# Two block layers on one core: every fourth copy of turned exponentials moved from ScalarE to VectorE

## What is computed

```
q = w8a8(x, wq, bq)                       # 16 heads of 32, 100 rows
k, v = cond @ wk.T + bk, cond @ wv.T + bv # 361 rows
scores = einsum(q, k) / sqrt(32) + mask
attn = softmax(scores)
out = w8a8(attn @ v, wo, bo)
```

## Time and profile before

| | us |
|---|---|
| median of 3 runs | 718.23 |
| lowest and highest | 718.14, 722.27 |
| profiled execution | 719.32 |
| its span, first to last instruction | 717.4 |
| attention's masks and exponentials, first to last | about 338 to 485 |
| VectorE's masks (line 1184) | 128 x 531 ns |
| ScalarE's exponentials (line 605) | 128 x 607 ns |
| ScalarE's copies of turned heads (line 596) | 128 x 405 ns |

### The profile page before, as it was taken

The page is one execution under the profiler, slowest core; times in us unless marked ns, Lnnn a source line. Parts: engine busy times, 40 slices in busy tenths (PEclk is TensorE's granted clock), DMA queues, the critical chain, the costliest instruction groups (busy, mean ns, idle before and its releaser), DMA issues. The chain is left out here.

```text
span 717.4 us, 11182 instructions
## 1 busy us (share of the span) xinstructions
PE 527.6 (74%) x3590; PEld 373.8 (52%) x3590; DVE 367.5 (51%) x962; ACT 296.6 (41%) x631; POOL 180.0 (25%) x211
## 2 busy tenths in 40 slices
PE   0070569999999999548999999994172089999991
PEld 0040557677777777323776666672172055555540
DVE  5727747755865766263578878762521032222220
ACT  4056623444344343042798888891010022222220
POOL 1001013222322321104244444423104502222221
PEclk9995779999999999859899999997555589999996
DMA  8959600000000000310122222421402524455534
GB/s 334 423 177 348 206 0 12 11 0 11 11 0 11 11 0 1 125 21 23 29 80 87 81 89 91 131 84 42 173 0 67 153 50 88 88 90 89 90 44 121
DMA packets 23076, 62.60 MB, mean 87 GB/s; under 512 B 3938, under 2 KB 9858, under 8 KB 20986
## 3 DMA queue, kind: packets, MB, share of 16 engines
q1 hardware_dynamic: 18622, 53.47, 22.1%
q0 software_dynamic: 4416, 8.63, 7.5%
HBM read 46.40 MB, written 17.32 MB: 89 GB/s over the span
## 5 line engine op out<-in xcount | busy, mean ns | idle before, releaser
L605 ACT ACTIVATE pE<-sN,nmx 100x361 f32<-100x361 f32 x128 | 77.7, 607 | 6.0 <-DVE nmx L1184 5.6
L1184 DVE CUSTOM_DVE_ANT_0 sN<-ps,maskS 100x361 f32<-100x361 f32 x128 | 61.9, 531 | 14.6 <-PE ps L793 6.1
L932 PE MATMUL ps<-VS,hTe 118*128 x120 | 56.7, 609 | 5.5 <-ACT hTe L643 5.5
L801 PE MATMUL ps<-ident,pE 100*121 100x100 f32 x384 | 57.5, 282 | 1.8 <-ACT pT L596 1.3
L801 PEld LDWEIGHTS ps<-ident,pE 100*121 100x121 f32 x384 | 47.5, 188 | 21.5 <-issue 20.4
L506 POOL DMA_INDIRECT sums_out<-yb,backI x20 | 31.1, 1554 | 108.2 <-ACT yb L653 104.4
L596 ACT COPY pT<-ps 121x300 f32<-121x300 f32 x128 | 51.8, 405 | 13.2 <-PE ps L801 12.6
L1296 DVE TENSOR_TENSOR hb<-ps,b1B 128x352 f32<-128x352 f32 x20 | 10.5, 524 | 87.6 <-PE ps L918 87.6
L918 PE MATMUL ps<-CT,xT 128*128 x160 | 52.5, 472 | 2.0 <-DVE xT L1282 2.0
L918 PEld LDWEIGHTS ps<-CT,xT 128*128 128x128 f32 x160 | 31.1, 196 | 24.7 <-issue 12.5
L1065 DVE TENSOR_REDUCE tk<-h 100x1 f32<-100x512 f32 x32 | 20.0, 680 | 39.6 <-ACT h L556 39.5
(11 more groups left out here) (237 smaller groups left out, 1181.5 us busy)
## 6 DMA issues: line engine op xcount, KB each, us to landing
VS<-in_w SPq DMA_DIRECT2D x8, 1024.0 KB, 9.1
CT<-in_ctxT SPq DMA_DIRECT2D x8, 728.0 KB, 16.4
CT<-in_ew SPq DMA_DIRECT2D x8, 704.0 KB
VS<-in_ew SPq DMA_DIRECT2D x8, 672.0 KB
slots_in<-zeros SPq DMA_DIRECT2D x5, 1056.0 KB, 12.4
xin<-slots_in SPq DMA_DIRECT2D x20, 264.0 KB, 3.4
XR<-in_x SPq DMA_DIRECT2D x1, 1600.0 KB
summB<-summary_rows SPq DMA_DIRECT2D x8, 200.0 KB
```

What stands on the lines that cost most here:

```text
L605: act.activation(pE[0:S, q, 0:T], sN[0:S, q, 0:T], ACT.Exp, scale=-1.0, bias=nmx[0:S, h_:h_ + 1], accum_out=sums[0:S, j, h_:h_ + 1]).then_ ...
L801: mm = pe.transpose(ps[0:TC, 4 + r, c * S:(c + 1) * S], pE[0:S, h_ % HPC, c * TC:(c + 1) * TC], ident[0:S, 0:S])
L932: mm = pe.matmul(ps[:, 7 - j, :], hTe[0:EC, 1 - j, c, :], vs(e)[0:EC, c * D:(c + 1) * D], start=(c == 0), stop=(c == 2))
L1184: dve.tensor_tensor_reduce(out=sN[0:S, q, 0:T], in0=ps[0:S, q, 0:T], in1=maskS[0:S, j, 0:T], scale=-1.0, scalar=3.4e38, op0=ALU.add, op1=A ...
```

## The change

ScalarE no longer copies the turned exponentials of the last head of a group (heads 3, 7, 11 and 15 of a batch). VectorE does, by a new function `copy_last`, right behind its mask of the head five later: that of head 3 behind mask 8, of 7 behind mask 12, of 11 behind mask 0 of the next batch, of 15 behind its mask 4. The last two of all come after the loop. The semaphores and the places in pT are the same; only the engine and the place in its order differ.

```diff
@@ ScalarE, body @@
                     at_turn = behind(b, h_ - TURN, first)
-                    if at_turn:
+                    if at_turn and at_turn[1] % HPC < HPC - 1:
                         copy_turned(*at_turn)
@@ ScalarE, after the batches @@
-            for ht in range(HEADS - TURN, HEADS):
-                copy_turned(B - 1, ht)
+            copy_turned(B - 1, HEADS - TURN)
@@ VectorE @@
+            def copy_last(b, ht):
+
+                n = b * 8 + ht // 2
+                dve.wait_ge(sem("p_turned1"), after(n + 1))
+                dve.wait_ge(sem("mixed"), groups_mixed(b * KC + ht // HPC - 1))
+                dve.tensor_copy(pT[0:TC, ht % (2 * HPC)].rearrange("p c s -> p (c s)"), ps[0:TC, 5, 0:NT * S])\
+                   .then_inc(sem("p_copied1"), 1)
+
@@ VectorE, body, behind the mask of head h_ @@
+                    if h_ % HPC == 0 and b * HEADS + h_ > 4:
+                        copy_last(*divmod(b * HEADS + h_ - 5, HEADS))
                     if h_ in steps:
@@ VectorE, after the batches @@
+            copy_last(B - 1, HEADS - 5)
+            copy_last(B - 1, HEADS - 1)
             finish5(B - 2)
```

## The result

| | before | after |
|---|---|---|
| median, us | 718.35 (6 runs, 717.7 to 722.3) | 767.8 (6 runs, 758.3 to 777.3) |
| ratio to before | | 1.058, 95% interval 1.052 to 1.065 |
| span of the profiled execution | 717.4 | 773.1 |
| VectorE's copies into pT | 0 | 32 x 466 ns |
| ScalarE's copies into pT | 128 x 405 ns | 96 x 405 ns |

The change makes the kernel about 6% slower.

The account below looks back on a forecast made before the run. The prediction took the ring TensorE to VectorE to TensorE as the bound: 719.3 us profiled + 21.4 order + 1.8 clock = 742.5, less 1.1 for the median = 741.4, rounded to 742; range 731 to 762.

Parts of the forecast that it names:

- Direction and mechanism: Attention stage: slower, chance 0.93, since TensorE's second turn of a group waits for VectorE's copy behind a mask needing new scores.
- The chain: From a group's scores through mask, gap and VectorE's copy to the second turn: 1.03 + 0.46 + 0.47 + 0.14 = 2.10 us.
- the late mask: Group of head 9: mask 12 comes 2.18 us after the scores, so the turn starts at 3.25 us.
- The other estimate, 0.44: VectorE's copy out of PSUM by the Trainium skill's formula, 120 cycles plus columns at 0.96 GHz: 0.44 us.
- The sum of the order: Delays of TensorE's groups over all batches: 10.2 + 6.3 + 3.1 + 1.8 = 21.4 us; a steady batch 18.9 to 21.5.
- the first group loses nothing: Steady batch, scores at 418.40: the next pass already waited for VectorE until 2.53 us after them; after the change 2.50, loss 0.
- ScalarE's relief: ScalarE loses 32 copies, 13 us of busy time, but was already waiting for TensorE, so nothing is gained.
- VectorE's load: VectorE gains 32 copies, 15 us; later masks shift about 0.45 us, covered by TensorE being 0.9 us late.
- The clock, one fall at 1.8 us: TensorE's clock falls to half once more in the attention stage, costing 4.5 - 4.5/1.7 = 1.8 us.
- the thin one: Stretch from the scores at 424.13: TensorE's scores 0.87 and two turns about 0.9 us busy of 3.4, a further fall likely.
- The steady stretch with 2.37 us busy: Kernel before: a TensorE stretch with 2.37 us busy kept the full clock, taken as evidence against frequent falls.
- rival 2: TensorE's clock falls about once a batch or oftener, every group holding idle time; seven falls 13 us, 748 to 765, chance 0.30.

Follow-up runs that it names:

- experiment 4: Changed kernel with VectorE's four copies moved behind the mask of the group's last head, four heads later instead of five: 724.9 us, ratio 1.006.
- experiment 1: Changed kernel with clock-holding products added on TensorE ahead of each group's second turn, filling the new waits: 743.5 us, ratio 1.035.
- experiment 2: Changed kernel with only head 3 of each batch copied by VectorE, ScalarE copying the other 15: 740.4 us, ratio 1.030.
- experiment 5: Kernel before, with ScalarE's copy of heads 3, 7, 11 and 15 cut to 4 of 300 columns, nothing new on VectorE: 719.6 us, ratio 1.000.
- experiment 9: Kernel before, ScalarE keeping all copies, with VectorE also copying 100x300 from PSUM into an unread scratch tile at the change's places: 722.1 us, ratio 1.003.
- experiment 11: The changed kernel itself, unaltered, run once more for a second profile: 758.9 us, ratio 1.057.
- experiment 8: Kernel before without its clock-holding products behind heads 5, 9 and 13 (HOLD = 0): 723.8 us, ratio 1.004.
- experiment 6: Kernel before, all copies on ScalarE, with VectorE adding two 100x300 tiles into an unread scratch tile at the change's places: 736.5 us, ratio 1.022.

## Why the prediction was right, and where it was not

- **Direction and mechanism: right.** The second turn of a group waits for VectorE's copy behind a mask that itself waits for scores issued just before. TensorE waited 30 times, 27.4 us. In another place of VectorE's order the same copies cost 5 us (experiment 4).
- **The chain, 2.10 us: measured 2.13; with the late mask 3.25: measured 3.25.** The copy, 0.47 from a line between two rows: 0.466. The other estimate, 0.44, was 0.03 short.
- **The sum of the order, 21.4 us: measured 22.9** (experiment 1). A batch 21.5: 21.78. The groups at full clock, 5.72, 5.83, 5.73 and 4.50 us, were forecast at 5.7, 5.6, 5.7 and 4.4. That the first group loses nothing is right for the change as a whole; with its copy moved alone it costs 1.2 us (experiment 2).
- **ScalarE's relief worth nothing: shown** (experiment 5). VectorE's load was put at nothing, since TensorE's lateness covers it; taken alone it costs 0.37 us a batch (experiment 9).
- **The clock, one fall at 1.8 us: the term that failed.** Both its price and its count were wrong. The price was read from rows that stop too early: the prediction let the half pace before run from 343.86 to 348.36, 4.5 us, while the turn at 343.03 already took 0.91 us and the products at 348.29 still took 1.52. It lasted about 6.5 us and cost 2.8, not 1.8 (experiment 1). In the changed kernel a stretch lasted 10 us and cost a batch 4.1 in experiment 11, and 13.84 and 5.5 in the first profile. And the falls came in every second steady batch, or in every one, not once. Together they are 16.2 us in experiment 11, and 33.2 in the first profile. The place was right: the prediction named the stretch behind the scores of head 12 as the thin one, and there it fell.
- The steady stretch with 2.37 us busy, which spoke against falls, has its 0.86 us of idle time in one piece, the new wait is 1.89. That the longer wait brings the falls is a reading that these kernels bear out only in part: falls stopped when the waits were filled (experiment 1), but three of six waits of 1.89 us in experiment 11 were followed by none, and in experiment 8 falls came behind 0.86 and 0.42.
- So rival 2, with the chance of 0.30, is what happened, except that the falls came behind one wait of a batch and not behind all. Its 748 to 765 holds the runs near 758. They also lie inside the range, which ended at 762, but by luck: that end was made of seven falls at 1.8 us and a copy of 0.69, and neither occurred. The point forecast of 742 comes close to the kernel of experiment 1, 743.5, in which the clock never falls, though the forecast counted a fall; the order's greater cost makes up for it. The median of 767.8 lies above the range.

What stays open: why the falls come in every batch in one profile and in every second in the other, and what besides the waits decides whether one comes. No run here was made for it.

## What to carry to other kernels

Before moving work to an engine with room, find what its place in that engine's order waits for: here the copy went behind a mask that needed the next scores, and 0.47 us of work made a wait of 0.8 to 1.9. An engine that is 86% busy may still only follow; cut its work alone and look whether the batch moves. Where TensorE is held at full clock by a dense schedule, price the new waits at the clock too, and take the price of a fall from rows that run from its first slow pass to its last. And first look for the bound elsewhere: one line moved on GpSimd gave 0.7%.

## What the runs showed of the hardware

- Half clock followed waits, but not each, and not by their length alone. Behind the wait of 1.89 us it came in six of six steady batches in the changed kernel's first profile and with head 7 alone, and in three of six in experiment 11; behind 2.0 us in four of five with head 3 alone; behind 1.50 in four of five with head 11 alone, and there once also behind 0.42 and 0.71 us (at 477.58 and 479.64). Products of no use put into the waits (21.20 us busy of 21.77) kept the full clock and made the kernel 15 us faster.
- VectorE's instructions that read SBUF tiles alone stretch beside GpSimd's: a 100x512 scaling from 0.48 to 1.27 us, a 100x300 addition from 0.47 to 1.32. Each time is the part that lies beside GpSimd's instruction plus a constant: for the scaling 0.98 + 0.28 us before, 0.60 + 0.28 in experiments 4 and 9, 0.37 + 0.28 in the changed kernel; for the addition of experiment 6, 0.98 + 0.33, 0.58 + 0.33 and 0.33 + 0.34. In these rows VectorE's instruction thus got nowhere until GpSimd's was over. The copies out of PSUM did not stretch: 0.46 to 0.47 in all kernels. The Trainium skill (GPSIMD Engine Reference, "Specifications") says that GpSimd shares its SBUF interfaces with VectorE, in contention with instructions that read two SBUF inputs or run in a two-port mode. The addition, with two inputs, agrees. The scaling reads one tile, and no run here shows its mode.
